# A selective-scan kernel: gates and row statistics moved off VectorE, to ScalarE and GpSimd

## The reference

```python
xz = einsum('bld,ed->ble', x, in_w); xs, z = split(xz, 2)
xc = silu(cb + sum(xp[:, k:k+L] * cw[:, k] for k in range(4)))     # convolution over 4 tokens
dt, Bm, Cm = split(einsum('bld,ed->ble', xc, xp_w), [16, 32])
delta = softplus(dt @ dt_w.T + dt_b);  A = -exp(A_log)
h = h * exp(delta*A) + (delta*xc) * B;  y = sum_n(h * C) + xc * D_skip   # token by token
y = y * silu(z)                                                    # the gate
x = layer_norm(y @ out_w.T + x) * ln_w + ln_b                      # each layer, then the next
```

## Time and profile before

| | |
|---|---|
| median of 3 runs | 8305.31 us (8304.15 to 8310.86) |
| the profiled execution's own time | 8300.88 us |
| its span, first to last instruction | 8299.1 us |
| granted TensorE clock, mean | 0.905 of full speed |
| VectorE, GpSimd, TensorE, ScalarE busy | 96%, 84%, 78%, 65% |

### The profile page before, as it was taken

The page is one execution under the profiler, slowest core; times in us unless marked ns, Lnnn a source line. Parts: engine busy times, 40 slices in busy tenths (PEclk is TensorE's granted clock), DMA queues, the critical chain, the costliest instruction groups (busy, mean ns, idle before and its releaser), DMA issues. The chain is left out here.

```text
span 8299.1 us, 74989 instructions
## 1 busy us (share of the span) xinstructions
PE 6477.3 (78%) x21028; PEld 2508.4 (30%) x21028; DVE 7941.7 (96%) x7922; ACT 5386.9 (65%) x8693; POOL 6969.2 (84%) x3380
## 2 busy tenths in 40 slices
PE   5778777777877777777777777777777777775888
PEld 2222222222222222222222222222222222222555
DVE  8999999999999999999999999999999999996777
ACT  5666676666666776667766667667666667663444
POOL 3898889988898888988899888988889888885555
PEclk8999999999999999999999999999999999987999
DMA  6444454444554454544544445454555445441110
GB/s 181 118 117 108 106 125 117 117 115 113 126 120 109 101 118 117 121 120 108 125 117 117 104 110 125 117 127 103 117 120 120 110 103 120 117 115 55 38 38 30
DMA packets 566552, 909.74 MB, mean 110 GB/s; under 512 B 58384, under 2 KB 200720, under 8 KB 564880
## 3 DMA queue, kind: packets, MB, share of 16 engines
q1 hardware_dynamic: 566160, 905.25, 45.5%
HBM read 716.08 MB, written 188.94 MB: 109 GB/s over the span
## 5 line engine op out<-in xcount | busy, mean ns | idle before, releaser
L890 POOL TENSOR_TENSOR hc<-h,crep 128x1024 f32<-128x1024 f32 x2048 | 4783.1, 2359 | 760.6 <-PE acc L473 672.7
L1009 DVE TENSOR_TENSOR_SCAN h<-dA,carry,bu 128x512 f32<-128x512 f32 x3072 | 3762.3, 1263 | 8.4 <-POOL hc L890 8.4
L628 ACT ACTIVATE dA<-drep,cur 128x512 f32<-128x512 f32 x4096 | 2618.1, 710 | 4.8 <-DMA drep<-delta_dram 3.5
L994 DVE TENSOR_TENSOR bu<-durep,B_all 128x1024 f32<-128x1024 f32 x2048 | 2477.2, 1210 | 97.4 <-PE B_all L455 63.3
L455 PE MATMUL B_all<-dtc,spread_b 128*128 128x512 f32 x2048 | 1326.8, 734 | 1556.3 <-DVE bu L994 1555.2
L637 ACT COPY carry<-h 128x4 f32<-128x4 f32 x1023 | 201.3, 197 | 2117.5 <-DVE h L1009 2115.9
L473 PE MATMUL acc<-hc,gather 128*32 128x512 f32 x8192 | 1273.1, 697 | 4.1 <-POOL hc L890 4.1
L1009 DVE TENSOR_TENSOR_SCAN h<-dA,bu 128x512 f32<-128x512 f32 x1024 | 1194.2, 1201 | 6.8 <-POOL hc L890 3.4
L497 PE MATMUL work<-xT,inw 128*128 128x512 f32 x2048 | 1027.9, 648 | 69.9 <-ACT xT L648 59.1
L455 PEld LDWEIGHTS B_all<-dtc,spread_b 128*128 128x128 f32 x2048 | 361.3, 209 | 2243.3 <-DVE bu L994 2182.8
L507 PE MATMUL work<-xs,taps 128*128 128x512 f32 x2048 | 957.1, 610 | 0.0
(11 more groups left out here) (176 smaller groups left out, 6667.3 us busy)
## 6 DMA issues: line engine op xcount, KB each, us to landing
drep<-delta_dram SPq DMA_DIRECT2D x1024, 256.0 KB, 6.0
durep<-du_dram SPq DMA_DIRECT2D x1024, 256.0 KB, 6.7
crep<-c_dram SPq DMA_DIRECT2D x1024, 64.0 KB, 6.4
delta_dram<-za SPq DMA_DIRECT2D x64, 1024.0 KB, 4.2
du_dram<-relu SPq DMA_DIRECT2D x64, 1024.0 KB, 5.3
x_in<-xbuf SPq DMA_DIRECT2D x64, 512.0 KB, 3.8
x_res<-xbuf SPq DMA_DIRECT2D x64, 512.0 KB, 3.8
xbuf<-x_res SPq DMA_DIRECT2D x64, 512.0 KB, 5.5
```

Source lines behind the costliest of these rows:

```text
L628: act.activation(dA[:, 4 * (s % 2) + k, :], drep[q % 2][:, k, :], ACT.Exp, scale=cur[:, p_, 4 * s + k:4 * s + k + 1]).then_inc(da_ready, 1)
L890: pool.tensor_tensor(hc[:, pair, :], h[:, pair, :], crep[:, j:j + 1, :].to_broadcast([P, 2, T]), ALU.mult).then_inc(hc_ready, 1)
L994: dve.tensor_tensor(bu[:, 2 * k:2 * k + 2, :], durep[q % 2][:, 2 * k:2 * k + 2, :], B_all[:].unsqueeze(1).to_broadcast([P, 2, T]), ALU.mul ...
L1009: dve.tensor_tensor_scan(h[:, r, :], dA[:, r, :], bu[:, k, :], start, ALU.mult, ALU.add).then_inc(scanned, 1)
```

## The change

The gate is split. ScalarE copies `acc` into a new buffer `sums` of two tiles (`take_sums`, which now signals `acc_read`), ahead of the exponentials in slots 6, 10, 14 and 2. GpSimd multiplies it by silu(z) after its products in the same slots (`gate`, which signals `gated`; the output projection waits for that).

The statistics are split as well. The output copy on ScalarE is done in four parts of 256 columns, each with its row sum. GpSimd turns the sums into minus the mean in slot 8 (`mean`), ScalarE squares the centred rows with a row sum in slot 9 (`squares`), and GpSimd makes the variance in slot 10. VectorE's gate, statistics and aggregation are gone.

To make room in SBUF, `x_in` is no buffer of its own: it lies in the first half of the xc buffer of the same chunk. Its load is issued in turn g for chunk g+2, behind the sums of slot 4, and stands ahead of the loads for the last quarter.

```diff
-        x_in = sb("x_in", [P, NT, D])
+        x_in = [xc[:, i, 0:2].rearrange("p e t -> p (e t)").rearrange("p (t d) -> p t d", t=NT) for i in range(2)]
+        sums = sb("sums", [P, 2, T])
...
             def load_x(n):
                 c = ready(n % CH)
-                if positive(n):
-                    sp.wait_ge(w_filled[1], fill(1, n - 1, "tr") + 1)
-                sp.dma_start(x_in[:], xv[c]).then_inc(x_loaded, 16)
+                if n >= 2:
+                    sp.wait_ge(summed, 2 * (NG * (n - 2) + QS) + 1)
+                sp.dma_start(x_in[n % 2], xv[c]).then_inc(x_loaded, 16)
...
                 if j == 0:
-                    pe.wait_ge(acc_read, DB * (m + 1))
+                    pe.wait_ge(gated, DB * (m + 1))
...
             def copy_out(m, j):
                 wait_filled(act, j, out_fill(j, m))
-                act.copy(x_res[:, 2 * j:2 * j + 2, :], W[j][:].rearrange("p (t d) -> p t d", t=2)).then_inc(w_read[j], 1)
+                for t in range(2):
+                    act.activation(x_res[:, 2 * j + t, :], W[j][:, t * D:(t + 1) * D], ACT.Identity,
+                                   accum_out=row_sum[:, 2 * j + t:2 * j + t + 1]).then_inc(w_read[j] if t else row_summed, 1)
+
+            def take_sums(n, q):
+                act.wait_ge(summed, 2 * (NG * n + QS * (q + 1)))
+                if positive(DB * n + q - 1):
+                    act.wait_ge(gated, DB * n + q - 1)
...
+                act.copy(sums[:, q % 2, :], acc[:]).then_inc(acc_read, 1)
+
+            def squares(m):
+                act.wait_ge(mean_ready, m + 1)
+                act.wait_ge(gated, DB * m + (DB + 1 if m < TOT - 1 else DB))
...
+                for t in range(NT):
+                    ins = act.activation(sums[:, t // 2, t % 2 * D:(t % 2 + 1) * D], x_res[:, t, :], ACT.Square, bias=minus_mean[:, t:t + 1],
+                                         accum_out=sq_sum[:, t:t + 1])
+                ins.then_inc(squared, 1)
...
+            def gate(n, p_, q):
+                if q == 0:
+                    pool.wait_ge(z_done, n + 1)
+                pool.wait_ge(acc_read, DB * n + q + 1)
+                pool.tensor_tensor(sz[:, p_, q, :], sums[:, q % 2, :], sz[:, p_, q, :], ALU.mult).then_inc(gated, 1)
...
+            def mean(m):
+                for j in range(2):
+                    pool.wait_ge(w_read[j], out_fill(j, m) + 1)
+                pool.tensor_tensor(minus_mean[:], row_sum[:], c_minus[:], ALU.mult).then_inc(mean_ready, 1)
+
             def variance(m):
-                pool.wait_ge(means, m + 1)
-                pool.tensor_tensor(ve[:], mv[:, :, 1], c_eps[:], ALU.add).then_inc(var_ready, 1)
-                pool.tensor_tensor(minus_mean[:], mv[:, :, 0], c_minus[:], ALU.mult)
+                pool.wait_ge(squared, m + 1)
+                pool.tensor_tensor(ve[:], sq_sum[:], c_over[:], ALU.mult).then_inc(newton, 1)
+                pool.wait_ge(newton, 6 * m + 1)
+                pool.tensor_tensor(ve[:], ve[:], c_eps[:], ALU.add).then_inc(var_ready, 1)
                 pool.wait_ge(var_ready, m + 1)
                 pool.tensor_tensor(half_ve[:], ve[:], c_half[:], ALU.mult).then_inc(newton, 1)
...
-            def statistics(m):
-                for j in range(2):
-                    dve.wait_ge(w_read[j], out_fill(j, m) + 1)
-                for t in range(NT):
-                    ins = dve.bn_stats(st[:, t], x_res[:, t])
-                ins.then_inc(stats, 1)
...
                     scan(at, ph, 0)
-                    if s == 2 and not is_first(g):
-                        gate(g - 1, other, DB - 1)
-                    if s in (6, 10, 14):
-                        gate(g, here, (s - 6) // 4)
                     times_b(at, 1)
```

More of the change, by code:

```diff
@@ L128, in mamba_layers @@
         carry = sb("carry", [P, NA])
-        st, mv = sb("stats", [P, NT, 6]), sb("mv", [P, NT, 2])
+        row_sum, sq_sum = sb("row_sum", [P, NT]), sb("sq_sum", [P, NT])
         ve, half_ve, minus_mean, lnv, guess, tmp, root, shift = (
             sb(n, [P, NT]) for n in ("ve", "half_ve", "minus_mean", "lnv", "guess", "tmp", "root", "shift"))
-        c_eps, c_half, c_minus, c_three = (sb(n, [P, NT]) for n in ("c_eps", "c_half", "c_minus", "c_three"))
+        c_eps, c_half, c_over, c_minus, c_three = (sb(n, [P, NT]) for n in ("c_eps", "c_half", "c_over", "c_minus", "c_three"))
         c_dram = nc.dram_tensor("c_dram", (2, 4 * QS, T), F32, kind="Internal").ap()
@@ L157, in mamba_layers @@
             sem(n) for n in ("da_ready", "bb_ready", "bu_ready", "scanned", "hc_ready", "summed", "carried"))
-        acc_read, stats, means, var_ready, lnv_done, guess_ready, newton, root_done, normed, weighted, x_ready = (
-            sem(n) for n in ("acc_read", "stats", "means", "var_ready", "lnv_done", "guess_ready", "newton",
+        acc_read, gated, row_summed, mean_ready, squared, var_ready, lnv_done, guess_ready, newton, root_done, normed, weighted, x_ready = (
+            sem(n) for n in ("acc_read", "gated", "row_summed", "mean_ready", "squared", "var_ready", "lnv_done", "guess_ready", "newton",
                              "root_done", "normed", "weighted", "x_ready"))
@@ L419, in turn @@
                     store_c(n, p_)
+                if not is_last(g) and not (isinstance(g, int) and g == TOT - 2):
+                    load_x(g + 2)
                 load_delta(g, 1 - p_, 3)
@@ L818, in turn @@
                     keep_states(group(g, s - 1))
+                    if s == 2 and not is_first(g):
+                        take_sums(g - 1, DB - 1)
+                    if s in (6, 10, 14):
+                        take_sums(g, (s - 6) // 4)
                     exp(group(g, s + 1), here if s + 1 < NG else other)
@@ L851, in turn @@
                     if not is_first(g):
+                        if s == 9:
+                            squares(g - 1)
                         if s == 11:
@@ L870, in _ @@
             turns(act, turn)
+            take_sums(TOT - 1, DB - 1)
             for j in range(2):
                 copy_out(TOT - 1, j)
+            squares(TOT - 1)
             root_guess(TOT - 1)
@@ L958, in turn @@
                     times_c(group(g, s))
+                    if s == 2 and not is_first(g):
+                        gate(g - 1, other, DB - 1)
+                    if s in (6, 10, 14):
+                        gate(g, 1 - other, (s - 6) // 4)
                     if not is_first(g):
+                        if s == 8:
+                            mean(g - 1)
                         if s == 10:
@@ L974, in _ @@
             turns(pool, turn)
+            gate(TOT - 1, 1, DB - 1)
+            mean(TOT - 1)
             variance(TOT - 1)
@@ L1139, in turn @@
                     times_b(nxt, 0)
-                    if s == 9 and not is_first(g):
-                        dve.wait_ge(stats, g)
                     scan(at, ph, 3)
[L1143 to L1147, removed]
-            turns(dve, turn)
[L1150 to L1154, removed]
+            turns(dve, turn)
 class Fp4:
```

21 lines of the change are left out of this document (12 added, 9 removed).

## The result

The changed kernel takes 8513.96 us (median of 4 runs, 8512.23 to 8517.03) against 8304.73 us before (4 runs). The ratio is 1.025, with a 95% interval of 1.0238 to 1.0263: 209 us slower, where 75 were forecast. The way was right, the size was not, and 8514 lies outside the range of 8265 to 8470.

The account below looks back on a forecast made before the run. The loop through ScalarE, GpSimd, TensorE and VectorE was taken as the bound: 114.1 us without waits plus 3.3 added makes 117.4 against 116.16 a turn, +75 us over 61 turns, so 8380 us, range 8265 to 8470.

Parts of the forecast that it names:

- What bounds the kernel: Loop through ScalarE, GpSimd, TensorE and VectorE takes 114.1 us without waits against 116.16 measured, so 2.0 us slack a turn.
- Rival 1: The loop isn't closed and VectorE stays the bound: the whole 256 us come in, 8050 us; chance 0.05.
- (a): ScalarE, end of slot 4 to GpSimd's first softplus product: 20.0 us, +0.47 for the copy of the sums in slot 6.
- (b): GpSimd, first softplus product to end of slot 12's first product: 43.9 us, +1.6 for a gate, the mean and variance.
- (c): GpSimd, from the end of slot 12's first product to the end of silu_xc: 36.1 us, +1.2 for one gate.
- (d): TensorE, from silu_xc through x projection and broadcast of B to VectorE's product for slot 4: 4.7 us, nothing added.
- The sum: Loop without waits 114.1 + 3.3 = 117.4 us a turn, +1.2 over 61 turns: +75 us, 8380 us.
- (e): VectorE, from its product with the broadcast to the end of slot 4: 9.4 us, nothing added.
- What stands beside: Work off the loop, such as gates of slots 2 and 6, squares and VectorE's stall in slot 8: costs nothing.
- rival 2: Loop 1.5 us shorter than worked out, VectorE's turn with its own stalls binds: 115.0 to 115.8, 8260 us; chance 0.11.
- The signs named: VectorE's busy share about 92%, its Mamba waits some 350 us; wrong if slot 2's projection takes over 4 us.
- Rival 4: TensorE falls to its lower clock in (d), projection 7.4 us: 4.7 us a turn more, 8670 us; chance 0.10.

Follow-up runs that it names:

- e1_copy_early: The changed kernel with ScalarE's copy of block 3's sums moved from the head of slot 2 into slot 1, behind the tanh; 8392.4 us.
- e2_xt_first: The changed kernel with ScalarE's copy of the transposed x in slot 11 moved ahead of the root's first guess; 8510.6 us.
- e4_three: e3_both with the copy of block 0's sums moved from the head of slot 6 to slot 5, ahead of the sigmoids; 8409.8 us.
- gates_only: The changed kernel with statistics and aggregation back on VectorE and the output copy in one instruction, so only the gates are moved; 8506.6 us.
- stats_only: The changed kernel with the four gates back on VectorE, reading PSUM, so only the statistics are moved; 8296.8 us.
- e3_both: The changed kernel with the edits of both e1_copy_early and e2_xt_first; 8402.6 us.

## Why the prediction was wrong, by its own steps

- **What bounds the kernel.** Right as far as the runs go. The loop through ScalarE, GpSimd, TensorE and VectorE with 2.0 us of slack is what decides, not VectorE's 96%. Rival 1 was well ruled out: none of the 256 us came in.
- **(a), +0.47.** Measured +0.66. The copy is 0.58 us long and 0.48 from start to start, as sized; the polynomial ends 0.50 us later than before. The rest is GpSimd's: it starts L938 0.32 us after the polynomial in the mean, against 0.14 before. In the turn shown its products of slot 6 started late, since they wait for TensorE's sums, and the skip product of slot 6 waits for ScalarE's copy as well. The gate behind them ran right up to the softplus product. The timeline of GpSimd:

```profile
4127.98 4.69 POOL L920 TENSOR_TENSOR hc<-h,crep 128x1024 f32<-128x1024 f32 x2 [5.84 <-PE acc L474]
4132.62 1.28 POOL L927 TENSOR_TENSOR sz<-sums,sz 128x512 f32<-128x512 f32 x1
4133.86 4.54 POOL L938 TENSOR_TENSOR quad<-quad,xs 128x2048 f32<-128x2048 f32 x1
```

  So the 2.32 us of idle time of the earlier trace rows, which were to cover the gate, were not there: ahead of L938 GpSimd stood 2.0 us in the mean before and 0.02 in the changed kernel.
- **(b), to 45.5.** Measured 45.58, with no wait in it.
- **(c), to 37.3.** Measured 37.28. The gate on GpSimd takes 1280 ns, 1.23 from start to start, where 1.2 was taken.
- **(d), "keeps its 4.7".** This is the step that failed. It was 6.69, and 2.0 us in 61 turns are 121 us of the 134 that were missing. e1_copy_early puts it back to 4.85 and gains 121.6. The prediction said that the skip product would start about 0.5 us later and the sums end at nearly the time of silu_xc, "where the margin is thinnest", and then priced that margin at nothing. Against silu_xc the skip product did start 0.58 us later (1.84 us ahead of its end in the mean, 2.42 before); but the sum needs it over 3 us ahead, since 3.19 us passed from its start to the projection's before. Three things kept it from getting there. The sum places VectorE at GpSimd's bound, where its scan of slot 14 comes 0.2 us behind the product of slot 12, as in e2_xt_first. Its own stall in slot 12 put it at 1.35 us there, and slot 15, at 7.61 us instead of 6.95, at some 1.8 us in all. And ScalarE's slot 1, 12.6 us from the states of slot 0 to the end of the copy, hangs on VectorE, so the copy came that much later too, while silu_xc hangs on GpSimd, which had not moved. The third is the clock: it stayed low from the skip product to the projection, which is 0.6 of the 2.0 us. These parts do not simply add up: e2_xt_first, without the stall of slot 12, gains 3 us. What a run gives a price for is the copy in its place, 121.6 us.
- **(e).** 9.28, as before.
- **What stands beside.** VectorE's stall of slot 12 was put at about 1 us (in rival 2) and slot 8's, for the exponentials, at 1 to 2 us. Measured from the length of the slots, less 6.95: 3.1 in slot 12, 2.0 in slot 7, 2.8 in slot 3, all for the broadcast of B. Slot 8 has no such stall (6.90 us), since the broadcast came late first, in slot 7. In e4_three, with block 0's copy moved, the stall of slot 7 is gone and the exponentials hold slot 8 for 1.2 us. That stalls beside the loop cost nothing by themselves was right in effect, by e2_xt_first.
- **The signs named.** VectorE's busy share fell to 90% and not 92%, and its waits in the Mamba part are some 560 us and not 350. The sign that was to tell a wrong forecast, a projection of over 4 us, did not appear: what failed was when it starts.
- **The rivals.** Rival 4 named the right place, (d), and a part of the cause at the wrong point. The projection took 3.80 us in the mean where 7.4 stood for the lower clock, so only 0.1 us of the clock is in it (in gates_only it was 4.48); the 0.6 us stand ahead of it, in the skip product and the sums. A rival "the copy holds TensorE in slot 2" was missing, though each of its terms stood in the text.
- **The sum.** 117.4 + 2.0 + 0.1 = 119.5 us a turn; the 0.1 is 0.2 in (a) and 0.1 in (b), less about 0.1 in (e).

## What to carry to other kernels

When work is taken off the busiest engine, follow the loop of dependences through all engines for one period, with the waits taken out, and compare its length with the period: the difference is all the slack there is, and what is put on the loop counts nearly in full once that is gone. Where a new wait is added to an in-order engine, ask what is queued behind the waiting instruction; here a skip product that nobody needed early held the projection and the broadcast behind it. And a list of waits doesn't say which wait is on the path: of two with 187 us each on TensorE, one was worth 122 us when only its slot 2 was mended (86.0 us are left in e1_copy_early), and the other was worth 3 when it was gone.

## What the runs showed of the hardware

- A row sum taken along with an activation on ScalarE is a second instruction. Groups by line in the changed kernel:

```profile
L737 ACT ACTIVATE x_res<-work 128x256 f32<-128x256 f32 x256 | 93.5, 372 | 21.4 <-PE work L536 21.4
...
L737 ACT ACTIVATION_READ_ACCUMULATOR x_res<-work 128x1 f32 x256 | 51.3, 200 | 0.0
```

  The reading takes 0.20 us, 0.09 of it from start to start. Two such halves cost 0.7 us against 0.47 for the one copy of 128x512, less than the 1.0 that I took from a form with SBUF input.
- A gate of 128x512 on GpSimd takes 1280 ns, on VectorE 665. The Trainium skill, GPSIMD Engine Reference, Engine selection, puts elementwise work with two inputs on GpSimd at about twice the time of VectorE. The trace agrees, with a ratio of 1.92, VectorE's gate reading one input from PSUM and GpSimd's both from SBUF. For the duration that rule (1.33 us) came nearer than my 1.2; for what the gate costs from start to start, 1.23 us, my 1.2 did.
- The projection took from 3.70 to 4.9 us over the turns of gates_only, in which TensorE waits between the broadcast and the skip product. In stats_only, which has no such wait, it was 3.70 in every turn. The copy's wait ahead of the skip product is what makes the lower clock last into it: e3_both differs from e2_xt_first by the place of the copy alone, and the projection took 3.74 us in the mean against 4.00. How far it lasts is open: the changed kernel has the same wait as gates_only, 187 against 182 us in all, and its projection took 3.80 against 4.48. Rival 4 had this part-way form.
